# Mean and variance of every second feed-forward tile from ScalarE's sums in place of VectorE's statistics

## What is computed

```python
def bitlinear(x, w):
    xn = layer_norm(x)                      # mean and variance over the row, eps 1e-6
    x_hat = absmax_quant(xn)                # clip(xn * 128 / max|xn|) * max|xn| / 128
    w_hat = ternarize_weights(w)            # sign(round(w / mean|w|)) * mean|w|
    return jnp.einsum('bsd,od->bso', x_hat, w_hat)
h = bitlinear(x, w_fc)                      # 512 -> 2048
h = jax.nn.gelu(h, approximate=False)
return bitlinear(h, w_proj)                 # 2048 -> 512
```

## Time and profile before

| | us |
|---|---|
| median of three runs | 1259.14 |
| the profiled execution, its own time | 1260.95 |
| its span in the trace | 1259.2 |
| VectorE busy | 1033.9 |
| TensorE busy (matmuls) | 1023.9 |
| ScalarE busy | 836.5 |
| GpSimd busy | 558.7 |

### The profile page before, as it was taken

One profiled execution on the slowest core, in us unless ns is written; L12 is line 12 of the kernel. 1 busy time (PEld: TensorE's weight loads), 2 busy tenths in 40 slices (PEclk: granted clock), 3 DMA queues, 4 the chain that ended last, 5 costly groups with the idle time before them and its releaser, 6 DMA issues.

```text
span 1259.2 us, 17217 instructions
## 1 busy us (share of the span) xinstructions
PE 1023.9 (81%) x5268; PEld 751.1 (60%) x5268; DVE 1033.9 (82%) x1399; ACT 836.5 (66%) x1577; POOL 558.7 (44%) x462
## 2 busy tenths in 40 slices
PE   5877887799678989789989756665789889879897
PEld 2234654468545566655658545554567667668776
DVE  5668787875899988799987879978999999997744
ACT  4753665564787775687885876681997878863332
POOL 1346523551446551356641413439646565552401
PEclk9778969899799987899989768787799999999998
DMA  5216632444324552324452252161001110100000
GB/s 191 83 37 185 175 93 92 126 146 131 92 82 137 176 167 62 105 75 153 151 186 74 69 199 69 52 234 46 18 30 35 46 33 23 30 14 9 17 18 17
DMA packets 59353, 115.80 MB, mean 92 GB/s; under 512 B 8880, under 2 KB 13232, under 8 KB 58240
## 3 DMA queue, kind: packets, MB, share of 16 engines
q1 hardware_dynamic: 59264, 114.70, 29.2%
...
## 4 chain that ended last, share of the span: by engine, by line
PE 42%; DVE 31%; ACT 10%; issue 9%; POOL 4%; DMA 1%; SPq 1%; DVEq 0%; ACTq 0%; POOLq 0%
PE ps L1670 6%; DVE hb L1773 6%; PE ps L1600 6%; PE ps L1753 5%; DVE y_acc L1795 5%; PE ps L1640 5%; PE ps L1743 4%; PE ps L1683 3%; PE ps L1614 3%; DVE du L1825 3%; DVE m_col L1870 2%; PE ps L1626 2%; ACT ps L1329 2%; PE ps L1653 2%; DVE fh L1999 2%
## 5 line engine op out<-in xcount | busy, mean ns | idle before, releaser
L1216 POOL TENSOR_TENSOR hb<-du,b_bc 128x1024 f32<-128x1024 f32 (+1 forms) x160 | 311.1, 1966 | 260.7 <-PE ps L1670 260.6
L1773 DVE TENSOR_TENSOR_SCAN hb<-ps,hb 128x1024 f32<-128x1024 f32 (+1 forms) x128 | 257.1, 2012 | 30.9 <-ACT ps L1329 22.3
L1329 ACT ACTIVATE ps<-delta,a_neg 128x511 f32<-128x511 f32 (+2 forms) x320 | 179.8, 597 | 72.5 <-DVE hb L1773 62.4
L1670 PE MATMUL ps<-ident,hb 128*128 128x128 f32 x1088 | 180.1, 305 | 58.8 <-DVE hb L1773 26.0
L1795 DVE SCALAR_TENSOR_TENSOR y_acc<-ps,ct,y_acc 128x512 f32<-128x512 f32 x256 | 183.4, 741 | 34.1 <-PE ps L1670 32.6
L1670 PEld LDWEIGHTS ps<-ident,hb 128*128 128x128 f32 x1088 | 139.2, 158 | 87.1 <-issue 43.8
L1443 ACT ACTIVATE p_q<-ps,m_col 128x512 f32<-128x512 f32 (+3 forms) x256 | 132.0, 523 | 50.2 <-DVE m_col L1870 43.8
L1640 PE MATMUL ps<-ident,p_q 128*128 128x128 f32 x640 | 107.0, 314 | 38.1 <-ACT p_q L1443 29.6
L1626 PE MATMUL ps<-k_st,q_st 128*128 128x512 f32 (+3 forms) x256 | 99.3, 431 | 36.8 <-ACT p_q L1443 24.3
L1460 ACT ACTIVATE p_t<-ps 128x512 f32<-128x512 f32 x160 | 89.8, 595 | 55.8 <-PE ps L1640 55.4
L1600 PE MATMUL ps<-xn_t,w_ring 128*128 128x512 f32 x256 | 119.2, 609 | 6.7 <-DVE tmp L1853 5.5
...
## 6 DMA issues: line engine op xcount, KB each, us to landing
...
q_st<-qk_d SPq DMA_DIRECT2D x128, 128.0 KB, 2.8
...
k_st<-qk_d SPq DMA_DIRECT2D x128, 64.0 KB, 2.3
...
```

Source lines behind the costliest of these rows:

```text
L1216: nc.gpsimd.tensor_tensor(piece_of(e, hi, lo).rearrange("p (a n) -> p a n", a=2), du[b % 2][:, 2 * h:2 * h + 2, lo:hi], b_bc[:, i % BC_RIN ...
L1329: ins = nc.scalar.activation(factors(j, hi, lo)[:, (hi - lo) * m + start:(hi - lo) * (m + 1)], delta[b % 2][:, et, lo + start:hi], ACT.Exp ...
L1670: mm = nc.tensor.transpose(Y[q % 2][:, P * et:P * et + P], piece_of(2 * r + et // 2, hi, lo)[:, at:at + P], ident[:])
L1773: v.tensor_tensor_scan(h, d, h, 0.0, ALU.mult, ALU.add).then_inc(scan_done, 1)
```

## The change

For odd t the gelu gets an accumulator output (the sum of its 512 values), ScalarE waits for its own write, and then squares the 512 gelu values from h_sb into the PSUM bank that the gelu has just read, with a second accumulator output. Only then `gelu_done` is raised. VectorE has no BN_STATS for these tiles; its `hstat` is one TENSOR_REDUCE that adds the four sums and the four sums of squares. GpSimd makes mean and variance of them with three instructions where one stood. Even tiles stay as they were.

Two waits are new: GpSimd's `xc` waits for the gelus of tile t - 4, ScalarE's gelu for `hstat` of tile t - 2. `follows` has new lengths: 1.5 for an odd gelu in place of 0.75, no VectorE share for it, 1.7 for GpSimd's `hstat` in place of 1.1.

```diff
--- before.py
+++ after.py
@@ -348,6 +348,11 @@
 T_NEEDS = [3, 3, 5, 5, 5]
 EMPTIED_BY = {"ln1b": "act", "inproj": "act", "xproj": "act", "ct": "act", "dt": "act", "v": "act", "pv": "act",
               "ot": "act", "on": "dve", "rot": "dve", "wo": "dve"}
+
+
+def sums_by_act(t):
+
+    return t % 2 == 1
 
 
 def y_reader(item):
@@ -526,12 +531,13 @@
         yield "sp", 1.6, [sp("x2store", *divmod(t, LT)), dve("proj", t - XF) if t >= XF else pe("pv", SLOTS // 2 - 1)]
     elif kind == "xa":
         t, = a
-        yield "dve", 1.2, [sp("fxload", t) if t < AHEAD else pool("xadd", B - 1, t % LT)] + ([pool("xa", t - 1)] if t else [])
+        yield "dve", 1.2, [sp("fxload", t) if t < AHEAD else pool("xadd", B - 1, t % LT)] + ([pool("xa", t - 1)] if t else []) \
+            + ([dve("xc", t - 4)] if t >= 4 else [])
         yield "pool", 2.4, [dve(*item)]
     elif kind == "xc":
         t, = a
         yield "dve", 1.9, [pool("xa", t), pe("xt", t - 2) if t >= 2 else dve("wo", B - 1, 1, 1)]
-        yield "pool", 1.5, [dve(*item), dve("wtot", 0)]
+        yield "pool", 1.5, [dve(*item), dve("wtot", 0)] + ([act("fc", t - 4, 3)] if t >= 4 else [])
     elif kind == "xt":
         t, = a
         yield "pe", 0.5, [pool("xc", t), dve("wo", B - 1, 1, 1)]
@@ -541,11 +547,12 @@
         t, n = a
         i = 4 * t + n
         yield "pe", 3.8, [dve("xt", t), dve("tern", 0, 3), act("fc", *divmod(i - 2, 4)) if i >= 2 else act("t", SLOTS - 1, 4)]
-        yield "act", 0.75, [pe(*item)] + ([pe("ht_ffn", t - 2, 3)] if t >= 2 else [pool("xadd", B - 2, LT - 1)] if t else [])
-        yield "dve", 0.7, [act(*item)]
+        yield "act", 1.5 if sums_by_act(t) else 0.75, [pe(*item)] + ([pe("ht_ffn", t - 2, 3)] if t >= 2 else [pool("xadd", B - 2, LT - 1)] if t else [])
+        if not sums_by_act(t):
+            yield "dve", 0.7, [act(*item)]
     elif kind == "hstat":
-        yield "dve", 0.35, [dve("fc", *a, 3)]
-        yield "pool", 1.1, [dve(*item)]
+        yield "dve", 0.35, [("act" if sums_by_act(a[0]) else "dve", ("fc", *a, 3))]
+        yield "pool", 1.7 if sums_by_act(a[0]) else 1.1, [dve(*item)]
     elif kind == "hn":
         yield "act", 1.3, [pool("hstat", a[0])]
         yield "dve", 1.3, [act(*item)]
@@ -800,6 +807,7 @@
         st_x = sb("st_x", [P, 2, 6])
         fh = sb("fh", [P, 4, 16])
         st_h = sb("st_h", [P, 2, 4, 6])
+        sum_h = sb("sum_h", [P, 2, 2, 4])
 
 
         early = base[0]
@@ -1278,12 +1286,21 @@
                     pool.wait_ge(fx_max, t + 1)
                     nc.gpsimd.tensor_scalar(x, x, f[:, 9:10], 1.0, ALU.mult, ALU.min).then_inc(xq_done, 1)
                     pool.wait_ge(gam_ready, 1)
+                    if t >= 4:
+                        pool.wait_ge(gelu_done, 4 * (t - 3))
                     nc.gpsimd.tensor_scalar(f[:, 12:13], f[:, 8:9], gam[:, 0:1], None, ALU.mult).then_inc(fx_scale, 1)
                 elif kind == "hstat":
                     t, = a
                     f = fh[:, t % 4]
                     pool.wait_ge(fh_var, t + 1)
-                    own.done(nc.gpsimd.tensor_scalar(f[:, 4:5], f[:, 1:2], EPS_Q, None, ALU.add))
+                    if sums_by_act(t):
+                        own.done(nc.gpsimd.tensor_scalar(f[:, 0:2], f[:, 0:2], 1.0 / FF, None, ALU.mult))
+                        own.settle()
+                        own.done(nc.gpsimd.tensor_scalar(f[:, 5:6], f[:, 0:1], f[:, 0:1], f[:, 1:2], ALU.mult, ALU.subtract))
+                        own.settle()
+                        own.done(nc.gpsimd.tensor_scalar(f[:, 4:5], f[:, 5:6], -1.0, EPS_Q, ALU.mult, ALU.add))
+                    else:
+                        own.done(nc.gpsimd.tensor_scalar(f[:, 4:5], f[:, 1:2], EPS_Q, None, ALU.add))
                     own.settle()
                     own.done(nc.gpsimd.tensor_tensor(f[:, 2:3], f[:, 4:5], neg_half[:, 0:1], ALU.pow))
                     own.settle()
@@ -1507,8 +1524,18 @@
                         act.wait_ge(tr_full, TURN["ht_ffn", t - 2, 3] + 1)
                     elif t == 1:
                         act.wait_ge(xadd_done, LT * (B - 1))
-                    nc.scalar.activation(h_sb[:, t % 2, 512 * n:512 * n + 512], F[BANK[kind, t, n]], ACT.Gelu,
-                                         scale=fx[:, t % 4, 12:13]).then_inc(gelu_done, 1)
+                    h = h_sb[:, t % 2, 512 * n:512 * n + 512]
+                    if sums_by_act(t):
+                        if t >= 2:
+                            act.wait_ge(fh_var, t - 1)
+                        own.done(nc.scalar.activation(h, F[BANK[kind, t, n]], ACT.Gelu, scale=fx[:, t % 4, 12:13],
+                                                      accum_out=sum_h[:, t % 2, 0, n:n + 1]))
+                        own.settle()
+                        nc.scalar.activation(F[BANK[kind, t, n]], h, ACT.Square, accum_out=sum_h[:, t % 2, 1, n:n + 1])\
+                            .then_inc(gelu_done, 1)
+                    else:
+                        nc.scalar.activation(h, F[BANK[kind, t, n]], ACT.Gelu, scale=fx[:, t % 4, 12:13])\
+                            .then_inc(gelu_done, 1)
                 elif kind == "wsum":
 
                     w, n = a
@@ -1990,8 +2017,12 @@
                 elif kind == "hstat":
                     t, = a
                     f = fh[:, t % 4]
-                    own.settle()
-                    v.bn_aggr(f[:, 0:2], st_h[:, t % 2]).then_inc(fh_var, 1)
+                    if sums_by_act(t):
+                        dve.wait_ge(gelu_done, 4 * t + 4)
+                        v.tensor_reduce(f[:, 0:2], sum_h[:, t % 2], AX.X, ALU.add).then_inc(fh_var, 1)
+                    else:
+                        own.settle()
+                        v.bn_aggr(f[:, 0:2], st_h[:, t % 2]).then_inc(fh_var, 1)
                 elif kind == "hn":
 
                     t, h = a
```

## The result

The change is slower. Its median is 1273.96 us (1269.1 to 1277.83, 4 runs), against 1258.8 us (1257.53 to 1260.72, 4 runs) of the kernel before on the same chip; the ratio is 1.0117, 95% interval 1.0075 to 1.0159. The forecast was 1256.1, from 1249 to 1264, so it missed the sign and the range. The profiled execution took 1276.43 us.

The account below looks back on a forecast made before the run. It took VectorE to bound the first stage, TensorE and each tile's chain the tail. Stage -4.0 and tail +1.0 make -3.0 us: 1257.95 from the profiled execution, 1256.1 us against the median, range 1249 to 1264.

Parts of the forecast that it names:

- ScalarE's 0.84 us per odd gelu: Odd tiles on ScalarE: accumulator reads and Square make the sums ready 0.84 us later than the gelu alone ended.
- GpSimd's 0.7: Odd tiles' statistics on GpSimd: three instructions in place of one add 0.7 us before hn.
- VectorE's 13.9: First stage: dropping odd tiles' BN_STATS and using a cheaper reduction makes VectorE 13.9 us lighter.
- four fewer table loads: First stage on ScalarE: the new order saves four table loads of 1.29 us, 5.2 us, counting the load without a drain.
- sum by stretch: Ten stretches between hn(0) and hn(10): the fullest engine of each adds up to 220.6 us, 1.0 less than 221.6.
- The first stage, -4.0 us: Feed-forward tiles among the last scans, hn(0) to hn(10): the stage gets 4.0 us shorter.
- is the bound: From 905 to 1131 us VectorE, busy 96% and idle 8.3 us in all, was taken as the bound.
- levelling (0.18): Rival, first stage: VectorE's idle time stays at 9 us, only its work counts; 1246 to 1251 us, chance 0.18.
- ScalarE's queue delays the scans: Rival, first stage: exponentials stand behind odd tiles' gelu, Square and read, and VectorE waits; about 1264.7 us, chance 0.21.
- point of decision: The delayed-scans rival decides once over 80% of ScalarE's added time turns up as VectorE idle time.
- The tail, +1.0 us: After hn(10): nothing covers GpSimd's added 0.7 us in tile 15; 1.0 us slower, 0.5 to 2.
- a sign of being wrong: The forecast would be wrong altogether if the tail moved by more than 2 us.

Follow-up runs that it names:

- run 3: The change's instructions in the order of the kernel before; 1272.58 us, ratio 1.0101.
- run 1: The kernel before plus an unused small tile that puts every later tile 64 bytes higher; 1258.98 us, ratio 0.9991.
- run 5: The kernel before, in its order, with the odd tiles' BN_STATS removed and no work added on ScalarE or GpSimd; 1257.73 us, ratio 0.9985.
- run 6: The kernel before, in its order, plus only ScalarE's gelu sums, wait and Squares; VectorE keeps BN_STATS; 1270.31 us, ratio 1.0093.
- run 9: The change without Square and the gelu's wait for itself, in the order of the kernel before; 1259.76 us, ratio 0.9994.
- run 15: The kernel of run 9 repeated to get a profile; 1257.5 us, ratio 0.9985.
- run 4: The instructions of the kernel before in the order of the change; 1270.29 us, ratio 1.0086.
- run 11: The instructions of the kernel before in an order planned with 0.80 us per gelu instead of 0.75; 1270.15 us, ratio 1.0082.
- run 12: The instructions of the kernel before in an order planned with 0.70 us per gelu instead of 0.75; 1269.45 us, ratio 1.0084.
- run 2: The change with its sums kept in the unused half of st_h, so that no tile moves; 1270.97 us, ratio 1.0086.
- run 7: The change's instructions for tiles 1, 3, 5, 7 and 9 alone, in the order of the kernel before; 1271.62 us, ratio 1.0093.
- run 10: The kernel before without the odd tiles' BN_STATS, in an order newly planned for that; 1268.84 us, ratio 1.0068.
- Run 13: The change in the order of before, each odd tile's four Squares together behind xq_hi, banks released at the gelu; 1275.29 us, ratio 1.012.

## Why the prediction was wrong

*The prices* were right. ScalarE's 0.84 us per odd gelu came as 0.84, Square 0.60 in the bounds, the reduction 0.154, GpSimd's 0.7 as 0.77, VectorE's 13.9 as 13.0 in the ten stretches. ScalarE's total there rose by 10.5 instead of 12 us. The four fewer table loads came (48 in the ten stretches where there were 52). The ten items of the sum by stretch add up to 220.8, not 220.6, which changes nothing.

*The rule on the table switch.* By the Trainium skill (ScalarE: Activation LUTs, What ACT_TABLE_LOAD costs) a switch costs a drain of about 1.38 us beside the load. In the rows of tile 7 a load starts 0.01 to 0.03 us after the work ahead of it, and the gelu 1.29 us after the load starts, in the kernel before and in run 3. No drain shows, so the measurement differs from the page and decides, and the sum was right to take the load alone.

*The first stage, -4.0 us, is the term that failed*: it measured +5.2 in the profile of the change, or +8.3 against run 1's stage. Two steps of it were wrong.

First, I said that VectorE, at 96%, "is the bound". Run 5 took 14.4 us off it and shortened the stretches by 3.8, or by 0.7 against run 1. I read this as VectorE following a loop through all engines: relieved, it waits for ScalarE's xq_hi and exponentials and for TensorE's y_out. By the ratio the free relief gives 2 us, and at most 4.4, so that the 4 us which I had forecast for the whole change are about all that its relief could give with no price paid. The gain was small, as the sums by stretch said, and of levelling (0.18) run 5 shows nothing.

Second, I took ScalarE's share over a stretch for its room. It is busy 79% of the stage, but much of its idle time lies ahead of hn, and around the last two gelus of tile 7 it has none: 1061.47 to the xq_hi in the kernel before. There each gelu's 0.84 us delays what VectorE waits for. I had this as the rival "ScalarE's queue delays the scans", with 0.21, and its point of decision: over 80% of ScalarE's added time turning up as VectorE's idle time. In the change's ten stretches 18 us of idle time are new, against 20 x 0.84 = 17 us of accumulators and Squares; in run 3, 19 against 15.5 measured. That is over the point, but the point was badly chosen: in run 5 the relief alone, with nothing on ScalarE, makes 10.6 us of new idle time. From run 5 to run 3 VectorE's idle time grows by 8.2 us for 15.2 of ScalarE, and in run 6 by 7.3 for 15.9, so about half turns up, not over 80%. The direction of the rival is what runs 6, 9 and 15 show. Its price, +5.6 us, was less than half of the 14.7 that the ratio gives: I had let the relief of 13.9 us stand against the waits, while run 5 shows that it is worth 2 us, and I had no term for the order.

The same page of the Trainium skill (ScalarE: Activation LUTs, Rules for kernel authors) says to multiply on VectorE, by the speed per element in bf16. The kernel that leaves these sums to VectorE is the faster one here: Square, its wait and the later bank on ScalarE cost some 1.1% (1.0101 against 0.9985 and 0.9994), and the BN_STATS on VectorE 0.15%, if anything. But the values are f32, no run squares on VectorE, and I read the loss as one of the place in ScalarE's queue, not of the price per element. So the page's reason is not tested.

*The order* was the part that I didn't see at all. I used the new order as an account of which work stands in which stretch, and took it to be as good as the old one. Runs 4, 11 and 12 put 0.8% on each of three new orders. The sum had no term for it, and no rival named it. A sign may have been that VectorE idles only 9 of 230.7 us, in an order that must fit the durations closely.

*The two halves don't add up* (1.0101 and 1.0086, together 1.0117). In the new order, which was made for ScalarE's longer gelus, the instructions cost 0.3% instead of 1.0%, and nothing by run 2 (1.0086, as run 4). I read this as the planner giving them room; no run shows it apart.

*The tail, +1.0 us.* From the last gelu of tile 15 to hn(15) it is 3.84 us where it was 3.07, the 0.7 forecast. Runs 3 and 7 put the tail's tiles at about 1 us, give or take 4. In the profiled execution the tail is +3.8, outside "0.5 to 2" and over the 2 us that I had named as a sign of being wrong; its granted clock is 0.94 against 0.97, and I had no term for that.

*The clock.* The granted clock, averaged over an execution, was 0.892 for the change (mean of 4) and 0.904 for the kernel before (mean of 17, beside runs 1 to 4); runs 3, 4 and 6 had 0.897. Through those 17, 0.01 of clock goes with 4.5 us (3.0 to 5.6 in the other groups). So of the 12.8 us between the two means some 5 go together with a lower clock and 7 to 8 remain at equal clock; this is a fit and no experiment. Which of clock and waits came first is open for the medians: no run changed the clock alone. In the stretches to tiles 3 and 7 the loss of the instructions stands at a clock of 1.00 in both kernels (runs 1 and 7).

*Open:* what makes the order of before better than its neighbours. The new ones spread their extra waiting over several waits of 1 to 5 us. In run 4, run 11, run 10 and the change the largest is VectorE's for ScalarE's hn (4.2, 4.2, 4.8 and 5.3 us, against 0.5 before); in run 12 it is that of y_out for TensorE (4.7). No run changes one of these alone. Open too is how the loss of the Squares divides among the waits. Run 13 has it with the bank free at the gelu, so the later bank is not needed for it; how much the bank adds in the change no run shows.
